# Spare matmuls inside the expert block and in the opening, staged row loads, an early load of x, and four edits to a step table: one Trainium2 core

## What is computed

```python
x = x + mamba(adapter(x, language))       # adapter: two small matmuls, layer norm
x = x + moe(cond2(x))                     # cond2: 9 gated feed-forward blocks, weighed

def mamba_layer(x):                       # 4 layers
    xz = layer_norm(x) @ Wi.T             # xs, z
    u = silu(conv4(xs)); dt, B, C = split(u @ Wx.T); dt = softplus(dt @ Wdt.T + b)
    h = exp(dt * A) * h + dt * B * u      # scan over the 128 tokens, 16 states a channel
    y = sum_s(h * C) + u * Dp
    return (y * silu(z)) @ Wo.T + x

def moe(x):                               # 8 experts of capacity 1024, two choices a token
    logits = x @ wg; f1, f2 = slots of the first and second choice
    disp[f1], disp[f2] = tokens           # rows scattered to the experts
    eo = gelu(disp @ w_gate) @ w_down     # per expert
    return g1 * eo[f1] + g2 * eo[f2]
```

## Time and profile before

| what | us |
|---|---|
| median of 3 runs | 2601.78 (2601.73 to 2603.53) |
| the profiled execution | 2602.57 |
| its span in the trace | 2600.8 |
| PE, DVE, POOL, ACT busy | 2339.2, 2047.0, 2050.7, 1609.3 |

### The profile page before, as it was taken

How to read it: one execution, slowest core, us unless ns; L and a number is a source line. 1 busy time by engine, 2 the same in 40 slices (tenths; PEclk the granted TensorE clock), 3 DMA queues, 4 the chain that set the end, 5 groups by cost and what they waited for, 6 DMA issues and landing times. The chain is left out here.

```text
span 2600.8 us, 22792 instructions
## 1 busy us (share of the span) xinstructions
PE 2339.2 (90%) x6094; PEld 1030.8 (40%) x6094; DVE 2047.0 (79%) x2011; ACT 1609.3 (62%) x2605; POOL 2050.7 (79%) x1264
## 2 busy tenths in 40 slices
PE   6688888888898889999999999999997999999994
PEld 4233333333333333333333333333333444444473
DVE  5799999999999999999999999999999243333121
ACT  3576777776777677777777777777775232232131
POOL 4599999999998899999999999999998233221266
PEclk9799999999999999999999999999999999999897
DMA  7455545564445766676667666766675400000533
GB/s 224 186 209 207 190 161 180 208 211 167 143 156 184 255 248 235 236 242 231 242 236 244 238 234 235 246 237 232 234 238 195 136 18 17 29 9 9 154 58 36
DMA packets 216931, 464.97 MB, mean 179 GB/s; under 512 B 29468, under 2 KB 109154, under 8 KB 216802
## 3 DMA queue, kind: packets, MB, share of 16 engines
q1 hardware_dynamic: 204818, 455.30, 51.6%
q0 software_dynamic: 11264, 7.98, 2.0%
q10 hardware_dynamic: 720, 0.23, 0.1%
HBM read 440.00 MB, written 23.99 MB: 178 GB/s over the span
## 5 line engine op out<-in xcount | busy, mean ns | idle before, releaser
L936 DVE TENSOR_TENSOR_SCAN hh<-decays,psdB 128x1024 f32<-128x1024 f32 x512 | 1165.9, 2283 | 62.0 <-ACT decays L736 20.3
L1075 POOL TENSOR_TENSOR products<-hh,Clo 128x1024 f32<-128x1024 f32 x408 | 962.6, 2363 | 94.1 <-DVE hh L936 93.2
L467 PE MATMUL psY<-products,ident 128*128 128x512 f32 x1674 | 824.8, 612 | 104.6 <-POOL products L1075 65.4
L736 ACT ACTIVATE decays<-dt,Acur 128x508 f32<-128x508 f32 x1024 | 667.7, 708 | 6.9 <-DVE hh L936 6.5
L467 PEld LDWEIGHTS psY<-products,ident 128*128 128x128 f32 x1674 | 306.8, 192 | 552.0 <-issue 358.4
L925 DVE TENSOR_TENSOR psdB<-psT,Blo 128x1024 f32<-128x1024 f32 x395 | 484.1, 1226 | 33.1 <-ACT psT L704 7.6
L1505 DVE TENSOR_TENSOR ac<-sg,d_bank 128x512 f32<-128x512 f32 x135 | 92.7, 688 | 222.9 <-PE d_bank L1352 204.2
L447 PE MATMUL psW<-xnT,wcur 128*128 128x512 f32 x496 | 227.5, 601 | 41.6 <-DMA diag<-diags_l 22.7
L1075 POOL TENSOR_TENSOR products<-hh,late 128x1024 f32<-128x1024 f32 x104 | 244.1, 2369 | 19.4 <-PE psY L467 19.4
L1079 POOL TENSOR_TENSOR products<-products 128x512 f32<-128x512 f32 x187 | 237.2, 1269 | 14.7
L1403 ACT ACTIVATE sg<-d_bank 128x512 f32<-128x512 f32 x135 | 80.6, 597 | 243.2 <-PE d_bank L1348 243.1
(11 more groups left out here) (219 smaller groups left out, 3061.8 us busy)
## 6 DMA issues: line engine op xcount, KB each, us to landing
Blo<-rows SPq DMA_DIRECT2D x280, 512.0 KB, 5.9
Clo<-rows SPq DMA_DIRECT2D x280, 512.0 KB, 5.1
late<-rows SPq DMA_DIRECT2D x104, 512.0 KB, 6.1
wcur<-taps_l SPq DMA_DIRECT2D x31, 512.0 KB
fw<-in_Wg SPq DMA_DIRECT2D x36, 256.0 KB, 5.3
fw<-in_Wu SPq DMA_DIRECT2D x36, 256.0 KB, 4.7
fw<-in_Wd SPq DMA_DIRECT2D x36, 256.0 KB, 5.5
disp<-fw SPq DMA_DIRECT2D x16, 528.0 KB, 7.3
```

Of the source, the lines that this page charges most:

```text
L467: ins = pe.matmul(psY[:, :], lhsT=ident[:, :], rhs=gg[k % NGB][:, j, :], start=False, stop=(k % NK == NK - 1 and j == last - 1))
L736: ins = act.activation(dA[k % NDA][:, j, :, 1:T], dt[i % 2][:, c, :, 1:T], ACT.Exp, scale=Acur[i % 2][:, s:s + 1])
L936: dve.tensor_tensor_scan(out=hh[k % NHB][:, :, :].rearrange("p c t -> p (c t)"), data0=dA[k % NDA][:, :, :, :].rearrange("p c q t -> p (c ...
L1075: ins = pool.tensor_tensor(gg[k % NGB][:, :, :], hh[k % NHB][:, :, :], tile(Clo, Chi, slot(i, s)), ALU.mult)
```

## The change

- Opening: x of group 0 is loaded right behind the ids, before the wait for them, on a semaphore of its own. `turn_x(0)` waits for that alone, and `hidden(0)` waits for the weights. TensorE runs 12 matmuls of 128x128 on the identity ahead of `turn_x(0)`.
- Wave block: `dtu1` goes from step 1 to step 3. From t = 2 on, variance plus eps and minus mean are made by ScalarE in step 10 (`split_moments`), ahead of `turn1`. `rstd` on GpSimd goes from step 6 to step 7, and `PAIRED` has step 6 in place of 7.
- Dense block: the 32 matmuls at its end, and the wait ahead of them, are gone.
- Expert block: TensorE runs 20 matmuls of 128x512 ahead of its first transposes. SyncE loads the first half of expert 0's rows, waits until it has landed, loads the second half, waits, loads expert 1, waits, and then loads the rest.

```diff
-ACT_AT = {1: ["dtu0", "params", "dtu1", "norm"], 2: ["turn0"], 4: ["sums1", "x0"], 5: ["x1"], 6: ["z0"], 7: ["z1", "silu"], 8: ["bcdt"], 10: ["turn1"], 11: ["dt0"],
+ACT_AT = {1: ["dtu0", "params", "norm"], 2: ["turn0"], 3: ["dtu1"], 4: ["sums1", "x0"], 5: ["x1"], 6: ["z0"], 7: ["z1", "silu"], 8: ["bcdt"], 10: ["moments", "turn1"], 11: ["dt0"],
-POOL_AT = {1: ["gate1"], 6: ["rstd"], 10: ["dt"], 11: ["dtu"], 12: ["gate0"]}
+POOL_AT = {1: ["gate1"], 7: ["rstd"], 10: ["dt"], 11: ["dtu"], 12: ["gate0"]}
-PAIRED = [0, 2, 3, 4, 5, 7, 8, 9, 13, 14, 15]
+PAIRED = [0, 2, 3, 4, 5, 6, 8, 9, 13, 14, 15]
...
 # SyncE, opening
                 sp.dma_start(ids[:, :], A["ids"]).then_inc(ids_ld, 16)
+                sp.dma_start(xg[0], A["x"][0:G].rearrange("b t d -> t b d")).then_inc(x0_ld, 16)
                 sp.wait_ge(ids_ld, 16)
                 load_adapter(0)
...
 # TensorE, opening
                 pe.wait_ge(cst, 1)
+                for r in range(12):
+                    pe.matmul(psW[:, 0:128], lhsT=ident[:, :], rhs=ident[:, :], start=True, stop=True)
                 turn_x(0)
...
 # ScalarE, step 10
+                def split_moments(t):
+                    act.wait_ge(moments, t + 1)
+                    act.wait_ge(rstd_ok, t)
+                    act.activation(vare[:, :], mv[:, :, 1], ACT.Identity, bias=K["eps"][:, 0:1])
+                    act.activation(negm[:, :], mv[:, :, 0], ACT.Copy, scale=-1.0).then_inc(rs, 1)
...
 # VectorE, statistics(t)
+                    at_least(dve, rs, 2 * t - 1)
...
 # GpSimd, deviation(t)
-                    pool.wait_ge(moments, t + 1)
                     at_least(pool, centred, t)
-                    pool.tensor_tensor(vare[:, :], mv[:, :, 1], K["eps"][:, :], ALU.add)
-                    pool.tensor_scalar(negm[:, :], mv[:, :, 0], -1.0, None, ALU.mult).then_inc(rs, 1)
+                    if t < 2:
+                        pool.wait_ge(moments, t + 1)
+                        pool.tensor_tensor(vare[:, :], mv[:, :, 1], K["eps"][:, :], ALU.add)
+                        pool.tensor_scalar(negm[:, :], mv[:, :, 0], -1.0, None, ALU.mult).then_inc(rs, 1)
...
 # TensorE, end of the dense block
-                pe.wait_ge(silued, CR + NST * NDT)
-                for r in range(32):
-                    pe.matmul(psG[r % 2][:, :], lhsT=ident[:, :], rhs=wgu[:, 0, 0, :], start=True, stop=True)
...
 # SyncE, expert block
                             sp.dma_start(dx[c][e][:, 0:HC, :], A["disp"][c, e, 0:CAP // NHT].rearrange("(n p) d -> p n d", p=128)).then_inc(x_first, 16)
+                        sp.wait_ge(x_first, 32)
...
                 for e in range(NE):
+                    if 0 < e < 3:
+                        sp.wait_ge(x_ld[BATCH[e - 1]], 32)
                     load_rows(e)
...
 # TensorE, expert block
+                for r in range(20):
+                    pe.matmul(psT[0][:, :], lhsT=K["ident"][:, :], rhs=K["fw"][:, 0, :], start=True, stop=True)
                 turn(0, 0)
```

More of the change, by code:

```diff
@@ L211, in wave_phase @@
             sem("a_" + n) for n in "xT_up xT_ok hid_up hid_ok cond_up cond_ok stats_ok var_ok rs h_ok neg".split())
-        a_st, pch, half_ln, half_dt, half_dtu = (sem(n) for n in "a_st pch half_ln half_dt half_dtu".split())
+        a_st, pch, half_ln, half_dt, half_dtu, x0_ld = (sem(n) for n in "a_st pch half_ln half_dt half_dtu x0_ld".split())
         ad_ld = [sem(f"ad_ld{p}") for p in range(NAB)]
@@ L245, in at_least, with rows_of @@
                 eng.wait_ge(sm, v)
+        def rows_of(g):
+            return 16 * (1 + G) * (g // NAB + 1) - (16 if g % NAB == 0 else 0)
         def residents(d):
@@ L272, in load_adapter @@
                     at_least(sp, h_ok, g + 1 - NAB)
-                    sp.dma_start(xg[p], A["x"][G * g:G * (g + 1)].rearrange("b t d -> t b d")).then_inc(ad_ld[p], 16)
+                    if g > 0:
+                        sp.dma_start(xg[p], A["x"][G * g:G * (g + 1)].rearrange("b t d -> t b d")).then_inc(ad_ld[p], 16)
                     for q in range(G):
@@ L404, in turn_x @@
                     p = g % NAB
-                    pe.wait_ge(ad_ld[p], 16 * (1 + G) * (g // NAB + 1))
+                    if g == 0:
+                        pe.wait_ge(x0_ld, 16)
+                    else:
+                        pe.wait_ge(ad_ld[p], rows_of(g))
                     at_least(pe, xT_ok, g - 1)
@@ L413, in hidden @@
                     pe.wait_ge(xT_ok, g + 1)
+                    if g == 0:
+                        pe.wait_ge(ad_ld[p], rows_of(0))
                     at_least(pe, hid_ok, g)
@@ L836, in _ @@
                                 act.preload_act_table_set(LNEXP)
+                            if what == "moments" and i + 2 < NIT:
+                                split_moments(i + 2)
                             if what == "centre" and i + 2 < NIT:
```

## The result

The changed kernel took 2608.58 us, the median of 11 runs (2604.91 to 2610.45). The kernel before took 2601.73 beside it (11 runs). The ratio is 1.0027, with a 95% interval of 1.0017 to 1.0036: slower by 6.85 us. I had forecast 2598.5 and a range that ended at 2607.0.

A forecast was written before the change was run, and what follows sets the result against it. No engine had room: a ring over several engines bound early iterations, VectorE paced late ones. Terms (-6.0, -0.4, +1.3, +1.8, rest 0) summed to -3.3 us: 2599.3, median 0.8 lower, so 2598.5; range 2591 to 2607.

The forecast's parts named there:

- The gap, -6.0: Dense block's end to first expert: transposes start 2.6 us earlier, take 0.5 less, up block 3.0 less; minus 6.0 us.
- Rival 5: Dense block's end: GpSimd held until scatters land (2.3 us) or longer, TensorE starts later; -1.0, 2600.8 us; chance 0.06.
- signs that I named for being wrong: An iteration gets shorter, the first up block takes over 5 us, or GpSimd waits for ScalarE in step 7.
- The opening, -0.4: Opening: x's issue ahead of the ids' wait makes later SyncE entries 0.4 us earlier, turn_x(2) near 22.6; minus 0.4 us.
- rival 3: Opening: the 12 matmuls warm TensorE and it stays so past 23 us; -6.8, 2595.0 us; chance 0.12.
- rstd in step 7, +1.3: Wave block, GpSimd: power and product between steps 7 and 8 add 0.1 us on the ring, 13 times; plus 1.3 us.
- Two operations ahead of turn1, +1.8: Wave block, ScalarE: they add 0.2 us ahead of a copy VectorE awaits in nine late iterations; plus 1.8 us.
- Rival 2: Wave block: ScalarE's pair takes 0.9 us, not 0.3, delaying step 8 and turn1; +9.1, 2610.9 us; chance 0.08.
- the rings: Wave block: waits chained over several engines, such as scan, GpSimd multiply, TensorE sums, ScalarE decays; delays there lengthen an iteration.
- dtu1, 0 and PAIRED, 0: Wave block: dtu1's copy goes into ScalarE's 3.91 us wait; PAIRED keeps the same number of adds; 0 us each.
- Rows in stages, 0: Expert block: staged rows arrive before they are wanted, covered by the spare matmuls; 0 us.
- the clause on the lost cover: Expert block: without the spare matmuls only the first row stage would be exposed, and that gets shorter.

The follow-up runs named there:

- e9_16_5: Kernel before with 16 spare matmuls in the dense block instead of 32, and 5 ahead of the expert block's first transposes: 2586.05 us, -16.0 us.
- e11_landed: Kernel before without the 32 spare matmuls; GpSimd waits for all scatters to land, then writes a small tile: 2591.91 us, one execution.
- e4_wave: Kernel before with the wave block's edits alone (dtu1, rstd with ScalarE's two operations, PAIRED): 2607.15 us, +5.7 us.
- e16_after_gap: Changed kernel with 16 spare matmuls in the dense block and 5, not 20, in the expert block: 2599.95 us, -1.8 us against the kernel before.
- e17_after_gap_nostage: Changed kernel with 16 and 5 spare matmuls and without the row stages: 2595.91 us, -5.3 us against the kernel before.
- e10_16_0: Kernel before with 16 spare matmuls in the dense block instead of 32, none in the expert block: 2590.53 us, -11.5 us.

## Why the prediction was wrong

**The gap, -6.0: the step that failed** was "the barrier falls to GpSimd, at 2419.3 plus the 0.3 us that separate TensorE's end from SyncE's first load". The 0.3 was TensorE's; GpSimd's own is 5.60. Before, its exit lay hidden under the 32 matmuls. Rival 5 named this place with 2.3 us and a chance of 0.06, and its working was right: TensorE started later one for one. With 5.6 instead of 0.3 the forecast gap is -0.7, within the spread of what was measured (+1.3 and -1.3). The other parts of the term held: the matmuls cost 19.1 us (forecast 20.2), the transposes 0.60, the up block 3.67. From the first output DMA to the end the changed kernel took 143.7 us, 143.6 before, so what is gained ahead of it counts in full here; in the kernels with the earliest experts a part is lost again (145.8 in `e9_16_5`). None of the signs that I named for being wrong looked at the barrier.

**The opening, -0.4:** measured +1.0, not told from no change. The step held (22.57). The 12 matmuls (3.2 to 8.7) make `hidden(0)` fast (eight records in 1.06 us, 1.91 before), but at 14.23 four transposes take 1.11 us again, so rival 3 fell as argued. At statistics 4 the six profiles with this opening have offsets of -2.26 to +1.76, the twelve others -1.98 to +0.02, so a single trace tells nothing of half a microsecond here. Most of that scatter arises behind the opening, from statistics 1 to 4: at statistics 1 the six stand at -0.50 to +0.13 and the twelve at -0.32 to +0.49. The means at statistics 4, +0.4 and -0.9, lean the way of the +1.0.

**rstd in step 7, +1.3:** right in kind and nearly in size: 0.08 us an iteration, 0.8 in all. In all eight profiles with it and the pair the offset grows by 0.5 to 0.8 from statistics 4 to 15, whether TensorE's level falls in these iterations or not. Of the nine with rstd in step 6, eight lie at -0.7 to +0.1, but `e11_landed`, with none of the wave block's edits, grows by 1.15: there the granted clock falls to 0.50 twice in each of these iterations. So one profile alone would not have shown the term.

**Two operations ahead of turn1, +1.8:** right in kind; 0.25 to 0.31 us a time and not 0.2, so 2.1 to 2.2. I took both operations to be like `parc` and `Acur`, started 0.09 us apart. The first, which adds a bias tile, takes 0.29 us and not 0.19, and the second starts 0.18 us behind it (947.71 and 947.89 in the first profile, the copy at 947.99). The overlap with the next operation is there as I had it; 0.28 us are added. Rival 2, a pair of 0.9 us, fell. The Trainium skill ("ScalarE: Activation LUTs", What ACT_TABLE_LOAD costs) gave an estimate of 0.28 us for the pair, and these offsets agree with it.

**What had no term: the loss from statistics 17 to 18**, 2.8 to 4.1 us in most executions. I costed PAIRED and the small operations on the rings alone, and never asked what they do to TensorE's level right after its idle stretch. In the profile of `e4_wave` it is the largest part of the wave block's 5.7 us: 0.8 + 2.1 + 2.8.

**dtu1, 0 and PAIRED, 0:** not told from no change (+1.2 and +1.3). `dtu1` went as written: its wait shrank from 5.03 to 0.98 us, and the next one grew from 3.91 to 7.11.

**Rows in stages, 0:** right in the changed kernel, under its 19 us of matmuls. Wrong in the clause on the lost cover: I looked at the rows, and it is the weights behind them that come late: TensorE waits 4.0 us for them, and the kernel gives 3.5 us back without the stages.

**Sum for a usual execution:** gap 0, opening about +1, rstd +0.8, pair +2.1, the loss +3: +6.9, against 6.85 measured. That the sum meets so closely is partly luck; the opening and the gap are each known to 2 us only, and whether TensorE's level falls at the start of the dense block moves a single execution by 2 us more.

## What to carry to other kernels

An engine that has never been last at a barrier has a release time that the trace does not show; bound it generously before you count what its predecessor's removal frees. Spare matmuls pay only in time that is dead anyway, up to the last microsecond before the real work: 16 and 5 gave 16 us (12 of them by the 32 being gone), 32 in one place cost 12. And when a wait goes into a queue, look at what stands last in that queue, not at what stands next.

## What the runs showed of the hardware

- GpSimd leaves a block 5.60 us after its last instruction ends (eight kernels, 5.60 or 5.61), whether its scatters have landed or not. TensorE's end released the same barrier in 0.3 us.
- TensorE kept the upper level over 1.6 us of idle time (`e9_16_5`, `e16_after_gap`), lost it after 2.0 us (`e17_after_gap_nostage`, from 2435.2 to 2438.6), and had lost it after 7.3 us (`e10_16_0`).
- At the start of the dense block the granted clock reads 0.50 for about 3 us in nine of nineteen profiles, whatever the edits, and the way from statistics 31 to the first scatter is then about 2 us longer (229.3 to 230.0 against 227.2 to 228.5).
- The granted clock reads 1.00 at 23 us in the kernel before, where four transposes take 1.12 us, and 0.50 at 22.6 us in the changed kernel, where they take the same 1.12. A 1.00 ahead of the first change in a record is no evidence; durations are.
